# A four-layer graph network on one core: store the transposed edge attributes, and apply the edge weights in every layer

## What is computed

```
e = edge_attr @ enc_edge_w + enc_edge_b
# each layer:
msg = relu(h[src] + e) + 1e-7
m = msg * t
alpha = softmax of m over the edges of one dst, channel by channel
agg = segment_sum(msg * alpha, dst)
out = h + agg, then a two-layer MLP with layer norms over the nodes
```

## Time and profile before

| | |
|---|---|
| median of 3 runs | 5297.16 us (5278.94 to 5298.56) |
| the profiled execution | 5282.58 us |
| its span, first to last instruction | 5280.6 us |
| mean granted TensorE clock | 0.673 of full speed |

### The profile page before, as it was taken

One profiled execution on the slowest core, in us unless ns is written; L12 is line 12 of the kernel. 1 busy time (PEld: TensorE's weight loads), 2 busy tenths in 40 slices (PEclk: granted clock), 3 DMA queues, 4 the chain that ended last, 5 costly groups with the idle time before them and its releaser, 6 DMA issues.

```text
span 5280.6 us, 39054 instructions
## 1 busy us (share of the span) xinstructions
PE 2419.4 (46%) x9927; PEld 1638.7 (31%) x9927; DVE 2887.4 (55%) x3862; ACT 1842.4 (35%) x3505; POOL 3084.4 (58%) x3248
## 2 busy tenths in 40 slices
PE   2566666765334444434433444344442443444444
PEld 1344444443322222223222222232232232222223
DVE  3566666666335555555634555555552555555555
ACT  1344443444223333333322333333332333333334
POOL 4666666653466666666355666666625666666661
PEclk8677676777566766666656667666665666666675
DMA  2344443434123333333313333333321333333332
GB/s 56 106 115 118 116 124 112 121 112 130 41 75 102 97 106 96 102 101 98 96 41 83 105 98 100 101 97 104 96 80 46 100 98 102 96 106 99 96 103 67
DMA packets 419248, 506.78 MB, mean 96 GB/s; under 512 B 184319, under 2 KB 190201, under 8 KB 419004
## 3 DMA queue, kind: packets, MB, share of 16 engines
q1 hardware_dynamic: 312398, 393.85, 23.2%
q0 software_dynamic: 103552, 109.52, 10.8%
q10 hardware_dynamic: 3054, 0.71, 0.1%
HBM read 216.36 MB, written 287.39 MB: 95 GB/s over the span
## 4 chain that ended last, share of the span: by engine, by line
another core or an unknown queue 43%; issue 18%; ACT 17%; DVE 11%; PE 10%; DVEq 1%; POOL 1%; ACTq 0%; DMA 0%; SPq 0%; POOLq 0%
PE pT L774 3%; ACT r L576 3%; ACT decay L583 3%; ACT sw_out L591 3%; DVE M L1057 2%; ACT pX L579 2%; PE pA L744 2%; DVE S L1071 2%; ACT u L578 2%; DVE W L1075 1%; DVE pR L1059 1%; DVE pR L1061 1%; PE pX L763 1%; PE pX L758 1%
## 5 line engine op out<-in xcount | busy, mean ns | idle before, releaser
L495 POOL DMA_INDIRECT zsrc<-z_rows,idx_all x3136 | 2986.9, 952 | 1864.3 <-issue 960.3
L774 PE MATMUL pT<-ident,S 128*128 128x128 f32 x1568 | 568.5, 377 | 2156.8 <-issue 1085.7
L1057 DVE TENSOR_TENSOR_SCAN M<-pR,M,u 128x512 f32<-128x512 f32 x392 | 502.3, 1281 | 1624.2 <-ACT u L578 1522.6
L774 PEld LDWEIGHTS pT<-ident,S 128*128 128x128 f32 x1568 | 337.0, 215 | 2229.9 <-issue 2198.4
L576 ACT ACTIVATE r<-pX 128x512 f32<-128x512 f32 x392 | 233.4, 595 | 2176.8 <-remote 1923.2
L1071 DVE TENSOR_TENSOR_SCAN S<-decay,S,pX 128x512 f32<-128x512 f32 x392 | 501.5, 1279 | 491.6 <-issue 369.8
L758 PE MATMUL pX<-e_in,ident 128*128 128x512 f32 x784 | 697.6, 987 | 118.1 <-ACT e_in L570 91.2
L763 PEld LDWEIGHTS pX<-ident,zsrc 128*128 128x128 f32 x3136 | 566.5, 253 | 405.8 <-issue 325.2
L591 ACT ACTIVATE sw_out<-pT 128x512 f32<-128x512 f32 x784 | 439.5, 589 | 713.4 <-issue 381.0
L763 PE MATMUL pX<-ident,zsrc 128*128 128x128 f32 x3136 | 540.5, 330 | 67.2 <-DMA zsrc<-z_rows,idx_all 67.2
L774 PE MATMUL pT<-ident,W 128*128 128x128 f32 x1568 | 541.4, 359 | 0.0
(11 more groups left out here) (175 smaller groups left out, 1968.7 us busy)
## 6 DMA issues: line engine op xcount, KB each, us to landing
sw_rows<-sw_out SPq DMA_DIRECT2D x784, 256.0 KB
e_in<-e_cols SPq DMA_DIRECT2D x300, 256.0 KB
zsrc<-z_rows,idx_all POOLq DMA_INDIRECT x3136
max_cols<-M SPq DMA_DIRECT2D x392, 128.0 KB
attr_in<-in_edge_attr_dram SPq DMA_DIRECT2D x196, 128.0 KB
e_cols<-e_in SPq DMA_DIRECT2D x98, 256.0 KB
z_rows<-z SPq DMA_DIRECT2D x25, 125.0 KB
node_sw<-sw_rows,row_idx POOLq DMA_INDIRECT x100
```

Source lines behind the costliest of these rows:

```text
L495: pool.indirect_dma_start(zsrc[c % RING][:, t4, h, :], None, z_rows, bass.IndirectOffsetOnAxis(idx_all[:, h, t4, c:c + 1].bitcast(U32), 0) ...
L774: last = pe.transpose(pT[b][:, at:at + P], scanned[c % 2][:, t4:CH:SUB], ident[:, :])
L1057: v.tensor_tensor_scan(M[s][:, 1:CH + 1], pR[s][:, :], u[s][:, :], M[s1][:, CH:CH + 1], ALU.add, ALU.max).then_inc(m_done, 1)
```

## The change

Layer 0 no longer makes the embedding. It copies the transposed attributes from `pA` into a ring tile `attr_t[c % 7]`, which takes the place of `e_in`, and that tile is what SP stores (`attr_cols`) and what layers 1 to 3 load. `add_edges` multiplies by `edge_w2` where it multiplied by the identity, in all layers, so the product goes straight into `pX`. The bias is added in the relu of `messages`, in all layers. `edge_linear` and `edge_embedding` are gone with their semaphores; the copy out of `pA` takes over the wait for the ring's buffer.

```diff
         attr_in = two("attr_in", [P, SUB, 2, H])
-        attr_t = sb("attr_t", [P, CH])
-        e_in = [sb(f"e_in{b}", [P, CH]) for b in range(RING)]
+        attr_t = [sb(f"attr_t{b}", [P, CH]) for b in range(RING)]
...
-                    sp.wait_ge(e_ready, c + 1)
-                    sp.dma_start(e_cols[c, :, :], e_in[c % RING][:, :]).then_inc(e_stored[c % RING], 16)
+                    sp.wait_ge(attr_sb, c + 1)
+                    sp.dma_start(attr_cols[c, :, :], attr_t[c % RING][:, :]).then_inc(cols_stored[c % RING], 16)
...
                 def attr_to_sb(c):
                     act.wait_ge(attr_tp, done(c))
-                    act.activation(attr_t[:, :], pA[:, :], ACT.Copy).then_inc(attr_sb, 1)
-
-                def edge_embedding(c):
-                    act.wait_ge(e_mm, c + 1)
                     if c >= RING:
-                        act.wait_ge(e_stored[c % RING], 16 * (c // RING))
-                    act.activation(e_in[c % RING][:, :], pA[:, :], ACT.Identity, bias=edge_b2[:, :]).then_inc(e_ready, 1)
+                        act.wait_ge(cols_stored[c % RING], 16 * (c // RING))
+                        act.wait_ge(x_mm, done(c - RING))
+                    act.activation(attr_t[c % RING][:, :], pA[:, :], ACT.Copy).then_inc(attr_sb, 1)
...
-                    act.activation(r[s][:, :], pX[s][:, :], ACT.Relu).then_inc(r_done, 1)
+                    act.activation(r[s][:, :], pX[s][:, :], ACT.Relu, bias=edge_b2[:, :]).then_inc(r_done, 1)
...
                 def attr_to_channels(c):
                     pe.wait_ge(attr_loaded[c % 2], 32 * (c // 2 + 1))
                     if c >= 1:
-                        pe.wait_ge(e_ready, c)
+                        pe.wait_ge(attr_sb, c)
...
-                def edge_linear(c):
-                    pe.wait_ge(attr_sb, done(c))
-                    pe.matmul(pA[:, :], edge_w2[:, :], attr_t[:, :], start=True, stop=True).then_inc(e_mm, 1)
...
                     if first_layer:
-                        pe.wait_ge(e_ready, c + 1)
+                        pe.wait_ge(attr_sb, c + 1)
...
-                    pe.matmul(pX[c % 2][:, :], ident[:, :], e_in[c % RING][:, :], start=True, stop=False, skip_group_check=True)
+                    pe.matmul(pX[c % 2][:, :], edge_w2[:, :], attr_t[c % RING][:, :], start=True, stop=False, skip_group_check=True)
...
                     if c >= 1:
                         back(c - 1)
-                    if first_layer and c + 1 < NCH:
-                        edge_linear(c + 1)
```

More of the change, by code:

```diff
@@ L80, in program @@
         max_cols = nc.dram_tensor("max_cols", (H, HALF), F32, kind="Internal").ap()
-        e_cols = nc.dram_tensor("e_cols", (NCH, P, CH), F32, kind="Internal").ap()
+        attr_cols = nc.dram_tensor("attr_cols", (NCH, P, CH), F32, kind="Internal").ap()
         rank_of = nc.dram_tensor("rank_of", (E,), I32, kind="Internal").ap()
@@ L198, in program @@
         dst_all = sb("dst_all", [NP, SB], I32)
[L199 to L203, removed]
+        dst_all_f = attr_t[0][0:NP, 0:SB]
+        is_node = attr_t[1][0:NP, 0:SB]
+        nth = attr_t[2][0:NP, 0:SB]
+        rank_part = attr_t[3][0:NP, 0:SB]
+        no_add = attr_t[4][0:NP, 0:SB]
         ones_col = sb("ones_col", [NP, 1])
@@ L246, in program @@
         attr_loaded = [sem(f"attr_loaded{s}") for s in range(2)]
-        e_loaded = [sem(f"e_loaded{b}") for b in range(RING)]
-        e_stored = [sem(f"e_stored{b}") for b in range(RING)]
+        cols_loaded = [sem(f"cols_loaded{b}") for b in range(RING)]
+        cols_stored = [sem(f"cols_stored{b}") for b in range(RING)]
         gathered = [sem(f"gathered{b}") for b in range(RING)]
@@ L253, in program @@
         attr_sb = sem("attr_sb")
-        e_mm = sem("e_mm")
-        e_ready = sem("e_ready")
         x_mm = sem("x_mm")
@@ L360, in load_attr, with load_cols @@
                     sp.dma_start(attr_in[c % 2][:, :, h, :], edge_rows(table, h, h * HALF_AT + c * CH)).then_inc(attr_loaded[c % 2], 16)
-            def load_e(c):
-                sp.dma_start(e_in[c % RING][:, :], e_cols[c, :, :]).then_inc(e_loaded[c % RING], 16)
+            def load_cols(c):
+                sp.dma_start(attr_t[c % RING][:, :], attr_cols[c, :, :]).then_inc(cols_loaded[c % RING], 16)
             def store_m(g0, c):
@@ L389, in first_layer @@
                 for c in range(AHEAD):
-                    sp.wait_ge(e_stored[c], 16 * USES)
+                    sp.wait_ge(cols_stored[c], 16 * USES)
                     sp.wait_ge(x_mm, done(NCH - RING + c))
-                    load_e(c)
+                    load_cols(c)
             def store_z(j):
@@ L409, in next_layer @@
                     sp.wait_ge(x_mm, done(g0 + (c - 1)))
-                    load_e((c + AHEAD) % NCH)
+                    load_cols((c + AHEAD) % NCH)
                     if c >= 1:
@@ L448, in _ @@
             for b in range(RING):
-                sp.wait_ge(e_loaded[b], 16 * ((L - 1) * USES + (1 if b < AHEAD else 0)))
+                sp.wait_ge(cols_loaded[b], 16 * ((L - 1) * USES + (1 if b < AHEAD else 0)))
             sp.wait_ge(out_stored, 16 * NG)
@@ L544, in _ @@
                 act.activation(node_t[j % 2][0:H, 0:w * NP], (pA, pH)[j % 2][0:H, 0:w * NP], ACT.Copy).then_inc(enc_sb, 1)
-            act.sem_inc(attr_sb, PRE)
             act.sem_inc(r_done, PRE)
@@ L595, in layer @@
                     attr_to_sb(0)
-                    edge_embedding(0)
                 for c in range(NCH):
@@ L602, in layer @@
                         copy_out(c - 1)
-                    if first_layer and c + 1 < NCH:
-                        edge_embedding(c + 1)
                     exps(c)
@@ L753, in add_edges @@
                     if first_layer:
-                        pe.wait_ge(e_ready, c + 1)
+                        pe.wait_ge(attr_sb, c + 1)
                     else:
-                        pe.wait_ge(e_loaded[c % RING], value(pe, (l - 1) * (16 * USES)) + 16 * (c // RING + 1))
+                        pe.wait_ge(cols_loaded[c % RING], value(pe, (l - 1) * (16 * USES)) + 16 * (c // RING + 1))
                     pe.wait_ge(sw_done, done(g0 + (c - 2)))
-                    pe.matmul(pX[c % 2][:, :], ident[:, :], e_in[c % RING][:, :], start=True, stop=False, skip_group_check=True)
+                    pe.matmul(pX[c % 2][:, :], edge_w2[:, :], attr_t[c % RING][:, :], start=True, stop=False, skip_group_check=True)
                 def add_nodes(c):
@@ L787, in layer @@
                     attr_to_channels(0)
-                    edge_linear(0)
                     pe.matmul(pH[0:NP, 0:NK], zeros_b[:, :], zeros_b[:, 0:NK], start=True, stop=False, **hist_mm)
```

## The result

| | before | after |
|---|---|---|
| median | 5290.49 us (5278.94 to 5298.56, 4 runs) | 5257.03 us (5254.31 to 5260.77, 4 runs) |
| profiled execution's span | 5280.6 us | 5257.2 us |

The ratio is 0.9939, 95% interval 0.9915 to 0.9962: faster by 33 us, or 0.6%. The forecast was 5236, with a range of 5165 to 5315.

A forecast was written before the change was run, and what follows sets the result against it. POOL's wait for `x_mm`, with PE's signals held, was taken as the bound. 5282.6 - 38 - 16 = 5228.6 us against the profiled execution, 5243 against the median; written as 5236, range 5165 to 5315.

The forecast's parts named there:

- POOL and its wait for `x_mm` as the bound: All layers: the pace follows POOL, and its wait for `x_mm`, 2.33 us a chunk in layer 0, can be won.
- PE's signals held during its bursts: PE's signals come out late while POOL issues gathers, and together about 2 to 3 us after it stops.
- The trip for the embedding is what keeps layer 0 at one chunk a burst: Layer 0: without it the nodes' add ends 5.6 us into POOL's burst, not 9.1, and POOL runs two chunks on end.
- 38 us from the pace: Layer 0: 12.375 us a chunk falls to 11.9, 0.475 us less, over 80 chunks.
- busy and short pauses stay 7.87 + 2.27 = 10.14: Layer 0: POOL's busy time and short pauses within bursts, in us a chunk, were taken as unchanged.
- 16 us at the end of layer 0: Layer 0 after the counting: 8 chunks gain 2.0 us each, from 13.64 to 11.6 us a chunk.
- After 1110 us: End of layer 0: a sign that the forecast is right would be no POOL wait above 5 us.
- The relu's bias at nothing: All layers: 0.09 us more per relu, 35 us of ACT over 392 if all on the path, priced at nothing.
- the 11.78: Layer 1's pace in us a chunk, expected to stay; another pace would show the relu or weights wrongly taken as free.
- The weights, SP: `edge_w2` for the identity: same shape and type, nothing; SP: one store a chunk as before, some 2 us earlier, no delay.
- an early signal gets out and a late one doesn't: Within POOL's burst: a signal 5.7 us after its start got out promptly, one at 9.1 us didn't.

## Why the prediction was right, and where it was off

- **POOL and its wait for `x_mm` as the bound; PE's signals held during its bursts.** Right. With a stop of 2.4 us in each chunk nothing is late, and with one in every second chunk, of either kind, the kernel gains; a longer ring makes it worse; on a chip that holds nothing the kernel before takes 949 us less. Why they are held the runs don't show.
- **The trip for the embedding is what keeps layer 0 at one chunk a burst.** Right. 42 waits of 3.2 us, relus 6.4 and 17.3 us apart, the add's end 5.6 us into the burst, all as written. Putting a matmul back costs 3 us, moving PE's work without taking the trip away costs 120. That the signal gets out at 5.6 us was in part luck, as said below.
- **38 us from the pace.** This is the term that was mis-sized. 0.335 us a chunk by 77 chunks is 26, of which 3.6 went in the first burst (the fourth relu is at 170.0, not at 166.4), and 20.7 were there at the 83rd relu. The step that failed is "busy and short pauses stay 7.87 + 2.27 = 10.14": they became (631.71 + 183.3) / 77.9 = 10.46. The waits did fall, from 2.33 to 1.74 us. (Both count one long stop behind the layer's first burst, 11.55 us before, which ends where the window begins, and 12.03 after. Without it they are 2.18 and 1.59, and 10.46 + 1.59 = 12.05 us is the pace.) A part of the 0.32 is the short pause between the two chunks of a pair, 2.35 us of pauses a chunk in place of 2.27. What grew otherwise are the gathers issued while DVE makes the one-hots of the counting, as the 1.67 us one at 592.79 beside the DVE instruction at 592.19; before, the like took 1.17 us. In the whole window there are 77 such gathers before and 78 after, and their excess over 0.945 us sums to 24.4 and 43.0 us. The Trainium skill, "GPSIMD Engine Reference", section Key points, says that GpSimd shares its SBUF interfaces with VectorE and contends with its instructions of two SBUF inputs; the one-hots' instruction is one, and the row agrees. Why more of it is met is open: it isn't that POOL issues on end, for with a stop in every chunk the excess is larger still, 71 us on 72 gathers.
- **16 us at the end of layer 0.** 14.8 to 16.0 (36.7 at the last relu, 1275.2 in place of 1311.9, less 20.7). After 1110 us the longest wait is 4.2 us, as was forecast.
- **The relu's bias at nothing.** Wrong: about 16 us lost against the same kernel without it, and 12 against before by one execution of each. The pace in layer 1's window, which was to show it, doesn't: (2545.4 - 1550.6) / 85 = 11.70 us, below the 11.78. The layers' whole lengths do. I reasoned that the add was finished 9.5 us before the relu that waits for it, so ACT was off the chain. But after a release ACT works off two chunks at once, and what it does there can still move the next add and with it the next release. That is argued: the runs give its price, and not the link of the chain through which it comes.
- **The weights, SP.** Nothing, as taken, as far as one execution of each can tell: without the bias, layers 1 to 3 take 2.6 us less than before.
- **How early a signal must come.** I took "an early signal gets out and a late one doesn't" as a time within the burst. The trace of before already speaks against it, in a chunk of layer 0 that I didn't read:

```profile
542.43 0.94 POOL L495 DMA_INDIRECT zsrc<-z_rows,idx_all  x1 [4.10 <-PE pX L763]
...
547.07 1.05 PE L763 MATMUL pX<-ident,zsrc 128*128 128x128 f32 x8
...
553.88 0.60 ACT L576 ACTIVATE r<-pX 128x512 f32<-128x512 f32 x1 [6.85 <-remote]
```

The add ends at 548.12, 5.7 us into POOL's burst, and is held until the burst is over. Of the six adds of the counting stage that end there, four were held, by 4.4 to 5.8 us; of those that end 5.5 to 6.2 us into a burst, 16 of 20 got out at once in after, but 6 of 24 in the run with the counting first. So the forecast had the right outcome on a rule that isn't right. The signals that come out one by one at a layer's start suggest a queue, in which what stands ahead of a signal counts; no run tests that, and what decides stays open.

The split by the marks: 5280.6 - 20.7 - 14.8 + 12.1 = 5257.2, for one execution of each kernel.

## What to carry to other kernels

Ask of a wait whether its releaser was late or its signal was: the earlier trace rows showed an add that ended 9.5 us before anything reacted, and taking work from PE ahead of it could not be expected to mend that. What pays then is to have fewer round trips between engines, since each may be held once, and the price of an operand added to an instruction on the releasing chain shouldn't be taken at nothing because the records before it show slack. And a gain that rests on such a hold holds only where the hold is: run on more than one chip before building on it.

## What was not expected of the hardware

- The hold differs by chip. With the same kernel four batches, on two chips, have medians of 5272 to 5290 us and one, on a third, 4341.53; a gather takes the same 945 ns there. I don't know what the chips differ in. The change itself wasn't timed where nothing is held; the nearest, the change with its bias as a matmul, came to 0.9988 of before.
- A held signal isn't let out by one short stop as a rule. With a stop of 2.4 us in every chunk nothing is late; with one in every second chunk many are late again, and at a layer's start two relus still stand 31.6 us apart.
- At the start of a layer, where POOL issues ten chunks without a stop, two relus stand 55.5 us apart (1398.49, 1454.02). The add that the second one waits for was over at 1399.62, by its record, 54.4 us before.
